# Second biases through TensorE into the attention's output bank, and a new order of the routing

## The chip, the cores and the metric

One core of a Trainium2 chip. The metric is the device time of one execution in microseconds (us); lower is better. Engines: TensorE (PE) multiplies matrices and writes PSUM, which has eight banks; VectorE (DVE) and ScalarE (ACT) do elementwise work and read PSUM; GpSimd (POOL) does elementwise work and issues the transfers with computed rows; SyncE (SP) issues most other transfers. Each engine works through its own list in order, and they wait for each other by semaphores.

## The reference

For 2048 tokens of 128 features (8 sequences of 256), with one layer norm shared by both branches:

```
xn  = layernorm(x)
out = x + linear_attention(xn) + moe(xn)

linear_attention: 16 heads of 8; phi(z) = elu(z) + 1
  Q, K, V = xn@Wq, xn@Wk, xn@Wv; Kv = phi(K)^T V; K1 = sum phi(K)
  (phi(Q) Kv) / (phi(Q) K1 + 1e-6), then @ Wo

moe: probs = softmax(xn @ gate_w^T + gate_b), top 2 of 8 experts
  h_e = relu(xn @ w1[e] + b1[e]); y_e = h_e @ w2[e] + b2[e]
  sum over the two chosen experts of prob_e * y_e
```

Everything is fp32; w1 is 128x256 and w2 256x128 for each expert.

## The kernel before

The tokens make 16 tiles of 128. The execution has these stages, which overlap.

**Routing.** x comes in five loads on SP's queue (parts of 2, 2, 4, 4, 4 tiles), followed there by constants, Wo and w2; identity, Wk|Wv|gate, Wq and the gate bias come on ScalarE's queue. VectorE takes the statistics, ScalarE the square roots, and three engines share the normalising (`xrow`). TensorE transposes, ScalarE copies back (`xT`), and `project_vg` (L923) makes V and the gate's logits for two tiles at a time. VectorE adds the gate bias, finds the top two (`top_two`, L642 and L645), and names the pair of experts (`find_pair`, L653 to L658, four tiles at a time). `rank_rows` (L948 to L955) counts on TensorE, in bf16, how many tokens of each pair stand ahead; `pair_starts` (L674) and `places` (L681 to L690) make of it each token's row in an order sorted by pair. `late_gates` (L731 to L744) makes the shares of tiles 8 to 15 on VectorE; GpSimd makes those of the first eight.

**Dispatch.** GpSimd scatters the 16 tiles of normalised rows to DRAM by these rows (L444), each row with its token number and its eight gate shares; SP then loads them back sorted (`xs`).

**Attention.** Per block of four tiles: `project_k`, `project_q`, ScalarE's exponential, VectorE's `finish_k` (L751) and `finish_q` (L756), `keys_values` (L992), VectorE's `mask_kv` (L761), `numerator` (L1007), VectorE's `divide` (L770 to L777), `transpose_att` (L1018), and `project_out`: an identity matmul puts x into the output's bank (L1031), four products with Wo add to it (L1036). ScalarE copies the sum out (`copy_sum`, L540) and SP stores it to `out`. phi of a key or query is max(min(exp(z), 1), z + 1); the 1 in z + 1 is put into the bank by an opener of one row of ones in bf16 (L935 for keys, L969 for queries), and the exponential takes it out again with a bias of -1.

**Visits.** In the sorted order each tile meets few experts; 59 visits (tile, expert) bound all cases. `visits` (L695 to L704) finds on VectorE which visits there are, `order_visits` (L976 on TensorE, L708 and L710 on VectorE) and `make_table` (L980) order them, `keep_table` (L715) keeps a table of offsets that the engines load into registers eight at a time. A visit is `first_product` (L1067), ScalarE's ReLU with b1 (L552), `second_product` (L1080), and on VectorE `take_y` (L793), which adds b2 from SBUF, and `accumulate` (L801), which adds the gate share times y to `acc`. The visits go through three banks each. Weights w1 are loaded anew for each visit, six buffers deep; w2 with b2 beside it is held whole.

**End.** When a tile's visits are done, GpSimd adds its rows to `out` by token number (`give_back`, L459). Tile s waits for the first `BOUND[s]` accumulations: 8, 16, 23, 28, 33, 37, 40, 43, and then two more for each tile up to 59.

The lists are written out by hand. TensorE's around the change: all value projections with `rank_rows(0)` and `rank_rows(1)` among them, key 1, rank 2, query 0, rank 3, key 2, query 1, kv 0, key 3, query 2, two warm-up matmuls, kv 1, kv 2, numerator 0, query 3, kv 3, warm-ups, numerator 1, warm-ups, and so on. Warm-ups are matmuls whose result nobody reads.

Of the kernel before, what the change touches and what calls it, by code (L numbers as in the profile page):

```python
# [11 lines left out]
ALU = mybir.AluOpType  # L12
# [3 lines left out]
P = 128  # L16
# [61 lines left out]
def linear_attention_with_pair_sorted_experts(nc, x, ident_in_dram, wkvg, wq, wo, gate_b, w1b, w2, consts,  # L78
# [13 lines left out]
    W1ROW = H + KC  # L92
    WROW = KC * D + D
# [12 lines left out]
    LATE = slice(8, T)  # L106
# [8 lines left out]
    with ExitStack() as ctx:  # L115
# [13 lines left out]
        wo_f = sb("wo_f", [P, D])  # L129
        gate_bias = sb("gate_bias", [P, E])  # L130
        w2_all = sb("w2_all", [P, E * WROW])
        w1_now = sb("w1_now", [P, NW, W1ROW])
# [13 lines left out]
        qf = sb("qf", [P, T * P])  # L146
        kf = sb("kf", [P, T, D])
# [21 lines left out]
        y = sb("y", [P, 2, D])  # L169
# [35 lines left out]
        vg_ps = [banks[:, (2, 3, 4, 6)[b % 4], 0:R * (D + E)].rearrange("p (r n) -> p r n", r=R) for b in range(B)]  # L205
        k_ps = [banks[:, i, :].rearrange("p (t d) -> p t d", t=4) for i in (7, 1, 0, 7)]
        rank_ps = banks[:, 5, 0:(T + 1) * NP].rearrange("p (t c) -> p t c", c=NP)
        order_ps = banks[:, 6, 0:1]
        table_ps = banks[0:3, 6, P:P + NI]
        kv_ps = [banks[:, i, :] for i in (6, 1, 6, 7)]  # L210
        num_ps = [banks[:, 2:4, :] if k % 2 == 0 else banks[:, 0:2, :] for k in range(NBLK)]
        attT_ps = banks[:, 4, :]
        wo_ps = [banks[:, 5 if k % 2 == 0 else 7, :] for k in range(NBLK)]
        warm_ps = banks[:, 5, 0:P]
        xsT_ps = [banks[:, n % 2, :] for n in range(len(XGROUPS))]
# [6 lines left out]
        gate_b_in = sem("gate_b_in")  # L222
        wkvg_in = sem("wkvg_in")
# [48 lines left out]
        y_done = sem("y_done")  # L272
# [52 lines left out]

        def group_of_visit(i):

            return sum(min(i // 2, T - 1) >= a for a, _ in XGROUPS) - 1
# [10 lines left out]
        def _(sp):  # L339
# [22 lines left out]
            def load_w1(i, woff):  # L362

                if i >= NW:
                    sp.wait_ge(h_done, KC * (i - NW + 1))
                sp.dma_start(w1_now[:, i % NW, :], w1b[:, bass.ds(woff, W1ROW)]).then_inc(w1_in[i % NW], 16)

# [16 lines left out]
        def _(pool):  # L384
# [17 lines left out]
            def shift(g):  # L402
                ts = blk_tiles(g)
                pool.wait_ge(top_done, 4 * g + 4)
                nc.gpsimd.tensor_tensor(shifted[:, ts, :], top8[:, ts, :], top8[:, ts, 0:1].to_broadcast([P, 4, 8]),
                                        ALU.subtract).then_inc(shift_done, 1)

            def gate_values(g):
                ts = blk_tiles(g)
                pool.wait_ge(rexpsum_done, g + 1)  # L410
                nc.gpsimd.tensor_tensor(gate2[:, ts, :], expd[:, ts, 0:TOP],
                                        rexpsum[:, ts].unsqueeze(2).to_broadcast([P, 4, TOP]), ALU.mult
                                        ).then_inc(gate2_done, 1)
                pool.wait_ge(gate2_done, g + 1)
                pool.wait_ge(chosen_done, g + 1)
                nc.gpsimd.tensor_tensor(gated[:, ts], chosen[:, ts],
                                        gate2[:, ts, :].unsqueeze(3).to_broadcast([P, 4, TOP, E]), ALU.mult
                                        ).then_inc(gated_done, 1)
                pool.wait_ge(gated_done, g + 1)
                nc.gpsimd.tensor_tensor(xrow[:, ts, D + 1:D + 1 + E], gated[:, ts, 0, :], gated[:, ts, 1, :], ALU.add  # L420
                                        ).then_inc(row_done, 1)
# [9 lines left out]
            def dispatch(t):  # L431
# [4 lines left out]
                if g < 2:  # L436
                    pool.wait_ge(row_done, g + 1)
# [30 lines left out]
            shift(0)  # L468
            shift(1)
            gate_values(0)  # L470
            gate_values(1)
# [9 lines left out]
        def _(act):  # L481
            nc.scalar.dma_start(ident_t[:], ident_in_dram).then_inc(ident_in, 16)
            nc.scalar.dma_start(wkvg_f[:], wkvg).then_inc(wkvg_in, 16)
            nc.scalar.dma_start(wq_f[:], wq).then_inc(wq_in, 16)
            nc.scalar.dma_start(gate_bias[:], gate_b.partition_broadcast(P)).then_inc(gate_b_in, 16)
# [23 lines left out]
            def exp_gates(g):  # L509
                if g < 2:  # L510
                    ts = blk_tiles(g)
                    act.wait_ge(shift_done, g + 1)
                    nc.scalar.activation(expd[:, ts, :], shifted[:, ts, :], ACT.Exp).then_inc(exp_done, 1)
# [4 lines left out]
            def copy_v(b):  # L518
                act.wait_ge(logits_done, b + 1)
                nc.scalar.copy(vext[:, R * b:R * b + R, 0:D], vg_ps[b][:, :, 0:D]).then_inc(v_done, 1)  # L520
# [54 lines left out]
            exp_gates(1)  # L575
            exp_k(0)
            for b in range(4, 7):
                copy_v(b)
            exp_k(1)
            copy_v(7)  # L580
            exp_q(0)
            exp_k(2)
            exp_gates(2)
# [3 lines left out]
            exp_q(3)  # L587
# [607 lines left out]
```

## Time and profile before

| | |
|---|---|
| median of 3 runs | 120.92 us (119.16 to 121.91) |
| the profiled execution's own time | 118.78 us |
| its span, first to last instruction | 117.0 us |
| busy in it: TensorE | 101.4 us (87%) |
| VectorE, ScalarE, GpSimd | 68.6, 60.5, 51.0 us |
| granted TensorE clock, mean | 0.973 |

The durations below come from the one profiled execution, whose own time is below the median. A busy TensorE is not TensorE at its peak: matmuls are pipelined and their ends are modelled, so the distance between starts says what one costs in a row. Rows of a timeline merge neighbours of one kind: the start, the time they cover, and their number. In brackets stands the idle time of the engine before it and what ended it.

### The profile page before, as it was taken

The page shows a single profiled execution, that of the slowest core. Times are in us where ns is not written, and L with a number is a line of the kernel's source. Part 1 is how long each engine was busy: PE and PEld are TensorE (multiplying, and loading weights), DVE is VectorE, ACT ScalarE, POOL GpSimd, SP SyncE. Part 2 cuts the span into 40 slices and gives each one's busy share as a digit, 9 for nine tenths or more (in the row PEclk, how much of TensorE's full clock was granted, in tenths as well). Part 3 has the DMA queues.
Part 4 walks back from the last instruction along what each step waited for, and adds up shares of the span by engine and source line. Part 5 has one row for each costly group of instructions (what it writes and reads, how often), then busy time and mean ns, then how long its engine had stood idle before and what let it go on. Part 6 is the DMA issues. An engine that isn't in the chain of part 4 may idle for free.

```text
span 117.0 us, 3091 instructions
## 1 busy us (share of the span) xinstructions
PE 101.4 (87%) x771; PEld 90.5 (77%) x771; DVE 68.6 (59%) x287; ACT 60.5 (52%) x171; POOL 51.0 (44%) x66
## 2 busy tenths in 40 slices
PE   6947989999797899989899999999999999999100
PEld 6946867667676777679899999999999999989000
DVE  0858988997719945011565556647567566574600
ACT  0657996444020221549466677776677667755000
POOL 5005800467777778011000403114505557887870
PEclk9999999999999999999999999999999999999955
DMA  3998000001111114999944665757577768962522
GB/s 93 279 339 365 11 0 6 0 24 48 54 63 57 48 55 128 250 252 346 311 110 127 131 165 145 174 136 171 162 162 161 185 154 165 198 112 23 45 22 25
DMA packets 16656, 15.52 MB, mean 133 GB/s; under 512 B 1920, under 2 KB 16256, under 8 KB 16512
## 3 DMA queue, kind: packets, MB, share of 16 engines
q1 hardware_dynamic: 13248, 12.88, 37.8%
q0 software_dynamic: 2816, 2.18, 12.9%
q10 hardware_dynamic: 576, 0.27, 0.8%
q8 instruction: 7, 0.11, 0.4%
q14 instruction: 9, 0.07, 0.2%
HBM read 12.09 MB, written 3.23 MB: 131 GB/s over the span
## 4 chain that ended last, share of the span: by engine, by line
issue 28%; PE 24%; POOL 19%; DVE 11%; DMA 10%; ACT 2%; POOLq 2%; SPq 1%; DVEq 0%
POOL out L459 19%; DMA x_tok<-in_x 5%; DMA out<-res 4%; PE banks L970 4%; PE banks L1031 3%; PE banks L1036 3%; PE banks L939 3%; PE banks L992 3%; PE banks L1007 2%; POOLq L115 2%; DVE att L777 1%; PE banks L923 1%; DVE idx L645 1%; PE banks L1018 1%; PE banks L969 1%
## 5 line engine op out<-in xcount | busy, mean ns | idle before, releaser
L552 ACT ACTIVATE h<-banks,w_now 128x128 f32<-128x128 f32 x118 | 36.9, 365 | 17.7 <-PE banks L1067 17.7
L459 POOL DMA_INDIRECT out<-acc,token x16 | 25.1, 1570 | 33.7 <-DVE acc L801 32.4
L1067 PE MATMUL banks<-xsT,w_now 128*128 x236 | 36.5, 278 | 0.7 <-DMA w_now<-in_w1b 0.4
L1080 PE MATMUL banks<-w_all,h 128*128 x236 | 36.1, 277 | 0.0
L1067 PEld LDWEIGHTS banks<-xsT,w_now 128*128 128x128 f32 x236 | 30.9, 192 | 1.4 <-issue 1.2
L1080 PEld LDWEIGHTS banks<-w_all,h 128*128 128x128 f32 x236 | 31.0, 192 | 0.3 <-issue 0.2
L793 DVE TENSOR_TENSOR y<-banks,w_all 128x128 f32<-128x128 f32 x59 | 17.2, 292 | 22.4 <-PE banks L1080 13.5
L801 DVE SCALAR_TENSOR_TENSOR acc<-y,xs,acc 128x128 f32 x59 | 20.7, 352 | 1.1 <-DVE y L793 0.9
L444 POOL DMA_INDIRECT sorted_dram<-xrow,slot x16 | 15.9, 991 | 5.3 <-issue 4.6
L895 PE MATMUL banks<-ones 128*128 128x128 f32 x42 | 7.4, 337 | 1.1 <-POOL ones L387 1.1
L895 PEld LDWEIGHTS banks<-ones 128*128 128x128 f32 x42 | 7.0, 250 | 1.5 <-POOL ones L387 1.1
L535 ACT COPY attT<-banks 128x512 f32<-128x512 f32 x4 | 2.3, 586 | 11.1 <-PE banks L1018 11.1
L530 ACT ACTIVATE qf<-banks,minus_one 128x512 f32<-128x512 f32 x4 | 2.8, 688 | 7.2 <-PE banks L970 7.2
L923 PE MATMUL banks<-wkvg_f,xT 128*128 128x136 f32 x32 | 5.0, 288 | 1.6 <-ACT xT L507 1.5
L609 DVE BATCH_NORM_STATS2 stats<-x_tok 128x6 f32<-128x128 f32 x16 | 3.6, 281 | 4.7 <-DMA x_tok<-in_x 4.5
L1007 PE MATMUL banks<-kv,qf 128*128 128x144 f32 x32 | 4.8, 294 | 1.6 <-DVE qf L756 1.6
L923 PEld LDWEIGHTS banks<-wkvg_f,xT 128*128 128x128 f32 x32 | 4.2, 190 | 2.3 <-issue 1.2
L1007 PEld LDWEIGHTS banks<-kv,qf 128*128 128x128 f32 x32 | 4.1, 190 | 2.1 <-issue 1.0
L1036 PEld LDWEIGHTS banks<-wo_f,attT 128*128 128x128 f32 x32 | 4.1, 191 | 2.1 <-issue 1.2
L396 POOL TENSOR_TENSOR xrow<-x_tok,mean_var 128x256 f32<-128x256 f32 (+1 forms) x3 | 1.6, 541 | 7.8 <-DVE rstd L617 7.8
L992 PEld LDWEIGHTS banks<-vext,kf 128*128 128x128 f32 x32 | 4.2, 190 | 1.0 <-issue 1.0
L786 DVE COPY xsT<-banks 128x256 f32<-128x256 f32 (+1 forms) x2 | 1.1, 554 | 6.1 <-PE banks L1050 6.1
(99 smaller groups left out, 115.4 us busy)
## 6 DMA issues: line engine op xcount, KB each, us to landing
w_now<-in_w1b SPq DMA_DIRECT2D x59, 129.0 KB, 2.7
w_all<-in_w SPq DMA_DIRECT2D x1, 1536.0 KB, 9.2
out<-res SPq DMA_DIRECT2D x4, 256.0 KB, 5.0
xs<-sorted_dram SPq DMA_DIRECT2D x3, 276.0 KB, 4.7
x_tok<-in_x SPq DMA_DIRECT2D x3, 256.0 KB, 6.1
xs<-sorted_dram SPq DMA_DIRECT2D x2, 138.0 KB, 3.3
x_tok<-in_x SPq DMA_DIRECT2D x2, 128.0 KB, 2.5
sorted_dram<-xrow,slot POOLq DMA_INDIRECT x16, 2.3
```

The lines of the kernel that those rows point to most:

```text
L444: nc.gpsimd.indirect_dma_start(out=sorted_dram, out_offset=bass.IndirectOffsetOnAxis(ap=slot[:, t:t + 1], axis=0), in_=xrow[:, t, :], in_o ...
L459: nc.gpsimd.indirect_dma_start(out=out_rows, out_offset=bass.IndirectOffsetOnAxis(ap=token[:, s:s + 1], axis=0), in_=acc[:, s * D:(s + 1) ...
L552: nc.scalar.activation(h[:, i % NH, c, :], h_ps[i % NHP][:, c * P:(c + 1) * P], ACT.Relu, bias=w1_now[:, i % NW, H + c:H + c + 1]).then_in ...
L793: nc.vector.tensor_tensor(y[:, i % 2, :], y_ps[i % NYP], w2_all[:, bass.ds(woff + KC * D, D)], ALU.add).then_inc(y_done, 1)
L801: nc.vector.scalar_tensor_tensor(out=mine, in0=y[:, i % 2, :], scalar=xs[:, bass.ds(goff, 1)], in1=mine, op0=ALU.mult, op1=ALU.add).then_i ...
L895: last = nc.tensor.matmul(warm_ps, ones[:], ones[:], start=True, stop=True)
L923: last = nc.tensor.matmul(vg_ps[b][:, r, :], xT[:, (R * b + r) * P:(R * b + r + 1) * P], wkvg_f[:, D:KVG], start=True, stop=True)
L992: last = nc.tensor.matmul(kv_ps[k][:, 256 * b:256 * b + NV], kf[:, t, :], vext[:, t, :], start=(r == 0), stop=(r == 1))
L1007: last = nc.tensor.matmul(num_ps[k][:, j // 2, (j % 2) * NV:(j % 2 + 1) * NV], qf[:, t * P:(t + 1) * P], kv[:, t // 2, :], start=True, sto ...
L1036: last = nc.tensor.matmul(wo_ps[k][:, j * P:(j + 1) * P], attT[:, t * P:(t + 1) * P], wo_f[:], start=False, stop=(j == 3))
L1067: last = nc.tensor.matmul(h_ps[i % NHP][:, c * P:(c + 1) * P], w1_now[:, i % NW, c * P:(c + 1) * P], xsT[:, bass.ds(toff, P)], start=True, ...
L1080: last = nc.tensor.matmul(y_ps[i % NYP], h[:, i % NH, c, :], w2_all[:, bass.ds(woff + c * D, D)], start=(c == 0), stop=(c == KC - 1))
```

## The change

- b2 leaves the visits: `take_y` is gone, and `accumulate` reads the product in PSUM. In its place the gate shares (tokens x experts) are written a second time (`gates`), transposed on TensorE four tiles at a time (`transpose_gates`), copied out by ScalarE (`copy_gatesT`), and multiplied in `project_out` with a block-diagonal b2 of 32 rows x 512 columns: one more fp32 product for each block, into the bank that already holds x.
- Queries have no opener: phi is min(exp(z), 1) + relu(z), with the ReLU as a second ScalarE operation for each block.
- Logits are taken for four tiles at a time, pairs named in groups of 8, 4 and 4 tiles, and the gate values of the first eight tiles in one step. The statistics of x's last two parts are taken in halves.
- Orders: see the lists in the diff. All `rank_rows` come after the value projections. The table of visits is made among the keys and queries, no longer between the divisions. ScalarE copies the last sum before the first sorted rows.
- Wq and the gate bias move from ScalarE's queue to SP's, behind the constants. Five of 21 warm-ups go.

```diff
@@ SP
             sp.dma_start(cst[:], consts).then_inc(consts_in, 16)
+            sp.dma_start(gate_bias[:], gate_b.partition_broadcast(P)).then_inc(gate_b_in, 16)
+            sp.dma_start(wq_f[:], wq).then_inc(wq_in, 16)
             sp.dma_start(wo_f[:], wo).then_inc(wo_in, 16)
+            sp.dma_start(b2_f[:], b2_blocks).then_inc(b2_in, 16)
             sp.dma_start(w2_all[:], w2).then_inc(w2_in, 16)
@@ ScalarE
-                nc.scalar.activation(qf[:, blk_cols(k)], q_ps[k], ACT.Exp, bias=minus_one[:, 0:1]
-                                     ).then_inc(qexp_done, 1)
+                nc.scalar.activation(qf[:, blk_cols(k)], q_ps[k], ACT.Exp).then_inc(qexp_done, 1)
+                nc.scalar.activation(q_relu[:, blk_cols(k)], q_ps[k], ACT.Relu).then_inc(qexp_done, 1)
...
+            def copy_gatesT():
+                act.wait_ge(gatesT_done, 1)
+                nc.scalar.copy(gatesT[:], gatesT_ps).then_inc(gatesT_copied, 1)
@@ VectorE: the visits
-            def take_y(i, woff):
...
-                nc.vector.tensor_tensor(y[:, i % 2, :], y_ps[i % NYP], w2_all[:, bass.ds(woff + KC * D, D)], ALU.add
-                                        ).then_inc(y_done, 1)
...
-                nc.vector.scalar_tensor_tensor(out=mine, in0=y[:, i % 2, :], scalar=xs[:, bass.ds(goff, 1)], in1=mine,
+                nc.vector.scalar_tensor_tensor(out=mine, in0=y_ps[i % NYP], scalar=xs[:, bass.ds(goff, 1)], in1=mine,
                                                op0=ALU.mult, op1=ALU.add).then_inc(acc_done, 1)
@@ VectorE: its list from the naming of the last pairs
             find_pair(2)
+            shares()
+            choose(0)
             late_shift()
-            finish_k(0)
             pair_starts()
             places(1, slice(0, 4))
+            finish_k(0)
+            finish_k(1)
             places(2, slice(4, T))
-            finish_k(1)
             mask_kv(0)
             finish_q(0)
-            choose(2)
-            choose(3)
+            choose(1)
             late_gates()
             finish_k(2)
+            visits()
             mask_kv(1)
             finish_k(3)
+            order_visits()
             finish_q(1)
             mask_kv(2)
+            keep_table()
+            divide(0)
             finish_q(2)
             mask_kv(3)
             finish_q(3)
-            divide(0)
             divide(1)
-            visits()
             divide(2)
-            order_visits()
-            keep_table()
             divide(3)
@@ TensorE
             def order_visits():
                 pe.wait_ge(table_step, 4)
-                pe.wait_ge(kvmask_done, 3)
+                pe.wait_ge(slot_done, 2)
...
             def project_out(k):
...
                 nc.tensor.matmul(wo_ps[k].rearrange("p (t d) -> p t d", t=4), ident_t[:], x_tok[:, blk_tiles(k), :],
                                  start=True, stop=False)
+                nc.tensor.matmul(wo_ps[k], gatesT[:, k * P:(k + 1) * P], b2_f[:], start=False, stop=False)
                 pe.wait_ge(attT_copied, k + 1)
@@ TensorE: its list from the last value projection
             project_vg(7)
+            rank_rows(0)
             project_k(1)
+            rank_rows(1)
+            project_q(0)
             rank_rows(2)
-            project_q(0)
-            rank_rows(3)
             project_k(2)
             project_q(1)
             keys_values(0)
             project_k(3)
             project_q(2)
-            warm_up(2, after=2)
+            order_visits()
             keys_values(1)
+            project_q(3)
+            make_table()
             keys_values(2)
             numerator(0)
-            project_q(3)
             keys_values(3)
-            warm_up(2)
+            transpose_gates()
             numerator(1)
-            warm_up(3)
+            warm_up(3, where=late_warm_ps)
             transpose_att(0)
             numerator(2)
-            order_visits()
             project_out(0)
             transpose_att(1)
-            make_table()
             numerator(3)
             project_out(1)
```

## Rows read from the trace of the kernel before

**Rows 1.** Busy time by stretch of the visits: engines, clock, DMA share, GB/s

```profile
60.00:80.00 20.00, 20.00 (x178) 19.98 (x179) 12.24 (x43) 13.56 (x44) 4.59 (x3) 1.00 0.60 147
```

**Rows 2.** VectorE's timeline: start, us, engine line op; accumulations of visits 42 and 58

```profile
96.22 0.35 DVE L801 SCALAR_TENSOR_TENSOR acc<-y,xs,acc 128x128 f32 x1
...
110.92 0.35 DVE L801 SCALAR_TENSOR_TENSOR acc<-y,xs,acc 128x128 f32 x1 [0.23 <-DVE acc L801]
```

**Rows 3.** TensorE's timeline: first visits, the seventh's first product, visit 42's second

```profile
51.79 1.12 PE L1067 MATMUL banks<-xsT,w_now 128*128 x8
...
57.76 0.71 PE L1067 MATMUL banks<-xsT,w_now 128*128 x4 [0.39 <-DMA w_now<-in_w1b]
...
93.55 0.61 PE L1080 MATMUL banks<-w_all,h 128*128 x4
```

**Rows 4.** GpSimd's timeline: scatters of tiles 7, 14 and 15

```profile
96.85 1.55 POOL L459 DMA_INDIRECT out<-acc,token  x1 [1.18 <-DVE acc L801]
...
110.17 1.56 POOL L459 DMA_INDIRECT out<-acc,token  x1 [0.41 <-DVE acc L801]
112.03 1.55 POOL L459 DMA_INDIRECT out<-acc,token  x1 [0.30 <-issue]
```

**Rows 5.** TensorE's timeline from the first ranking to the sorted rows

```profile
14.34 0.36 PE L948 MATMUL banks<-zero_bf,ones_bf 128*128 128x476 bf16 x1
...
15.29 0.62 PE L923 MATMUL banks<-wkvg_f,xT 128*128 128x136 f32 x4
...
18.46 0.38 PE L935 MATMUL banks<-ones_bf 1*128 1x512 bf16 x1
...
21.79 0.39 PE L935 MATMUL banks<-ones_bf 1*128 1x512 bf16 x1
...
28.67 2.13 PE L992 MATMUL banks<-vext,kf 128*128 128x144 f32 x16
31.65 1.22 PE L1007 MATMUL banks<-kv,qf 128*128 128x144 f32 x8 [0.85 <-DVE qf L756]
...
36.46 1.22 PE L1007 MATMUL banks<-kv,qf 128*128 128x144 f32 x8 [0.79 <-DVE qf L756]
...
40.29 0.38 PE L976 MATMUL banks<-visited,cst 128*128 128x1 f32 x2 [0.52 <-DVE visited L704]
...
44.17 1.02 PE L1031 MATMUL banks<-x_tok,ident 128*128 128x512 f32 x2
45.03 1.05 PE L1036 MATMUL banks<-wo_f,attT 128*128 128x128 f32 x8
...
50.78 0.38 PE L1050 MATMUL banks<-ident,xs 128*128 128x128 f32 x2
```

**Rows 6.** All engines' timeline: GpSimd takes the first sorted rows

```profile
50.63 0.19 POOL L451 CAST token<-xs 128x2 uint32<-128x2 f32 x1 [4.26 <-DMA xs<-sorted_dram]
```

**Rows 7.** VectorE's timeline: end of the third part's statistics, start of the fourth's

```profile
6.45 0.36 DVE L612 BATCH_NORM_AGGREGATE mean_var<-stats 128x2 f32<-128x6 f32 x4
8.26 0.87 DVE L609 BATCH_NORM_STATS2 stats<-x_tok 128x6 f32<-128x128 f32 x4 [1.44 <-DMA x_tok<-in_x]
```

**Rows 8.** VectorE's timeline: scan of pairs, third key finish, second mask, table of visits

```profile
22.45 0.21 DVE L674 TENSOR_TENSOR_SCAN start_of<-ones,banks 128x28 f32<-128x28 f32 x1
...
28.05 0.68 DVE L751 SCALAR_TENSOR_TENSOR kf<-kf,banks 128x512 f32<-128x512 f32 x1
29.86 0.46 DVE L761 TENSOR_TENSOR kv<-banks,cst 128x288 f32<-128x288 f32 x1 [1.13 <-PE banks L992]
...
39.25 0.23 DVE L695 TENSOR_SCALAR ends_in<-start_of,cst 128x28 f32<-128x28 f32 x1
```

**Rows 9.** Busy time by stretch after the last matmul; TensorE's granted clock after POOL's column

```profile
108.50:109.00 0.50, 0.02 (x1) 0.00 (x0) 0.49 (x2) 0.00 (x0) 0.50 (x1) 1.00 1.09 100
...
110.00:110.50 0.50, 0.00 (x0) 0.00 (x0) 0.40 (x2) 0.00 (x0) 0.33 (x1) 1.00 0.46 17
110.50:111.00 0.50, 0.00 (x0) 0.00 (x0) 0.27 (x2) 0.00 (x0) 0.50 (x1) 0.66 0.99 111
```

More of the change, by code:

```diff
@@ L324, in normalised, with pairs_known @@
             return [sum(len(n) for n in norm[:i + 1]) for norm in (NORM_DVE, NORM_ACT, NORM_POOL)]
+        def pairs_known(t):
+            return sum(t >= a for a, _ in PAIR_GROUPS)
         def group_of_visit(i):
@@ L423, in fill_rows @@
+                nc.gpsimd.tensor_tensor(gates[:, EARLY, :], gated[:, EARLY, 0, :], gated[:, EARLY, 1, :],
+                                        ALU.add).then_inc(gates_done, 1)
             def fill_rows():
@@ L587, in _ @@
             exp_q(3)
+            copy_gatesT()
             copy_attT(0)
@@ L605, in _, with statistics @@
         def _(dve):
-            def statistics(i):
+            def statistics(i, half=None):
+                a, b = PARTS[i]
+                if half is not None:
+                    a, b = a + 2 * half, a + 2 * half + 2
                 dve.wait_ge(x_in[i], 16)
-                for t in range(*PARTS[i]):
+                for t in range(a, b):
                     nc.vector.bn_stats(stats[:, t, :], x_tok[:, t, :]).then_inc(stats_done, 1)
-                for t in range(*PARTS[i]):
+                for t in range(a, b):
                     dve.wait_ge(stats_done, t + 1)
@@ L745, in late_gates @@
                                         ).then_inc(row_dve_done, 1)
+                nc.vector.tensor_tensor(gates[:, LATE, :], gated[:, LATE, 0, :], gated[:, LATE, 1, :], ALU.add
+                                        ).then_inc(gates_dve_done, 1)
             def finish_k(k):
@@ L889, in _, with warm_up @@
         def _(pe):
-            def warm_up(times, after=0):
+            def warm_up(times, where=warm_ps):
                 pe.wait_ge(ones_set, 1)
-                if after:
-                    pe.wait_ge(slot_done, after)
                 for _ in range(times):
-                    last = nc.tensor.matmul(warm_ps, ones[:], ones[:], start=True, stop=True)
+                    last = nc.tensor.matmul(where, ones[:], ones[:], start=True, stop=True)
                 last.then_inc(pe_warm, 1)
@@ L951, in rank_rows @@
                 pe.wait_ge(pair_done, g + 1)
[L952 to L954 removed]
+                a, b = PAIR_GROUPS[g]
+                nc.tensor.matmul(rank_ps[:, a:b, :], before_bf[:], of_pair[:, a:b, :], start=False, stop=False)
+                for t in range(a, b):
                     last = nc.tensor.matmul(rank_ps[:, t + 1:T + 1, :], ones_bf[:, 0:P],
@@ L994, in keys_values, with transpose_gates @@
                 last.then_inc(kv_done, 1)
+            def transpose_gates():
+                pe.wait_ge(table_done, 1)
+                pe.wait_ge(gates_done, 1)
+                pe.wait_ge(gates_dve_done, 1)
+                for k in range(NBLK):
+                    last = nc.tensor.transpose(gatesT_ps[:, k * P:(k + 1) * P],
+                                               gates[:, blk_tiles(k), :].rearrange("p t e -> p (t e)"), ident_t[:])
+                last.then_inc(gatesT_done, 1)
             def numerator(k):
```

244 lines of the change are left out of this document (114 added, 130 removed).

## The prediction

> **What bounds the kernel now.** I read the table by stretches first, then the engines' timelines. The execution has two halves, and each has its own bound.
>
> The visits, from 51.8 us on: TensorE is busy for 20.00 of 20.00 us, with 178 instructions [rows 1]. A visit is eight of them, so it takes 20.00 / 22.25 = 0.90 us. VectorE, with a bias add and an accumulation for each visit, must be read against that. Counted back from the last, the accumulation of visit 42 (of 0 to 58) starts at 96.22 [rows 2], its second product on TensorE already at 93.55 [rows 3]. With 0.61 us for the product and 0.35 for the accumulation, VectorE's result comes 96.57 - 94.16 = 2.4 us after TensorE's. TensorE's pace is not slowed by it, but GpSimd's is: the scatter of tile 7 needs visits 0 to 42 and starts 0.28 after that accumulation, at 96.85; the last one starts at 112.03 [rows 4]. Back to back one takes 1.86 us (110.17 to 112.03), eight make 14.9 of these 15.2 us. So the end is set by GpSimd's queue, and that by visit 42.
>
> The attention, up to 51.8: TensorE's last product ends at 50.78, where the transposes of the sorted rows start [rows 5]; the first sorted rows have landed at 50.63 [rows 6]. Two chains arrive together. Whatever lengthens TensorE's one moves the visits; shortening the dispatch alone gives nothing.
>
> **The change, part by part.** All times are on the profiled execution's own clock.
>
> *Visits and end.* The bias add goes, and one of VectorE's three register loads with it. VectorE then finishes an accumulation some 0.5 us after TensorE's product: 0.14 to start and 0.36 to run. The accumulation from PSUM is not in the trace; bounds are the 0.35 us from SBUF [rows 2] and that plus another half, which moves the result by 0.2. I take the near one. Tile 7's scatter starts 2.4 - 0.5 = 1.9 earlier, and eight scatters back to back lose the 0.25 of pauses between them: -2.15. Nothing at the end can take more, since GpSimd then waits for nothing but itself.
>
> *Front.* Two small loads move from ScalarE's queue to behind x on SP's, and the 1.5 MB of w2 starts three issues later. VectorE had finished the third part's statistics by 6.81 and waited for x's fourth load until 8.26, 1.44 us [rows 7]. With less beside it that load can land before 6.8; bounds are a gain of 1.4 and none, and I take the first. The Trainium skill (DMA: Bandwidth & Descriptors, Issuing engines are not separate DMA queues) says that transfers started by different engines run on the same DMA engines and interleave; by that rule the moved loads did hold x up, and the gain is 1.4, without it none. No run here shows it yet.
>
> The halved statistics give back some 0.1 of it, as ScalarE's next square root waits for both halves. More is lost on TensorE: ranking now stands behind all value projections. Before, these end at 18.46 and the last ranking at 21.79, 3.33 us with a key and a query projection between. Now the first half of the ranking, 0.95 us for its first group (14.34 to 15.29) and about 0.6 for its second, comes in there too, and one query opener goes, 0.39 as the key's at 21.79 has the same shape [rows 5]: 3.33 + 1.55 - 0.4 = 4.5. So ranking ends at 18.46 - 1.4 + 0.1 + 4.5 = 21.65, and VectorE's scan, at 22.45 before [rows 8], starts at 21.85: 0.6 earlier. Dispatch gains this 0.6 and no more.
>
> *The wait that the new order brings.* Instruction order on TensorE is now: second query projection, kv(0), third key and query projections, ordering of visits, kv(1). The ordering matmul waits for VectorE's visit table, and behind it in TensorE's queue stand kv(1), the fourth query, kv(2) and all numerators. VectorE's list up to there: from the scan to the end of the third key finish 6.2 us before (22.45 to 28.05, and 0.6) [rows 8], now with the first key finish inside it (0.6) and a second sum of the gates (0.2); then the table and its hand-over to TensorE, 1.04 (39.25 to 40.29) [rows 5, 8]. 21.85 + 6.2 + 0.8 + 1.0 = 29.85. TensorE is there at 21.65 + 1.4 + 0.95 + 1.0 + 1.35 + 0.95 = 27.3 (key, query, kv, key, query) and waits some 2.6 us.
>
> Then the two engines alternate. Ordering to 30.1; VectorE's mask 1.19 after kv(1)'s start (28.67 to 29.86) at 31.3; mask, key finish and order step 1.45, to 32.7; table matmul 0.2; kv(2) at 32.95, numerator(0) 1.0 later. The first division ends 2.8 after that numerator's start, 36.75, and two query finishes and a mask, 1.6, put the fourth query at 38.3. Numerator(1) waits for it: 38.45, against 36.46 [rows 5]. That is +2.0, although the front gave 0.6. The extra ReLU of the queries costs nothing while ScalarE idles there.
>
> *TensorE's own work after it.* From numerator(1) to the end, before: 50.78 - 36.46 = 14.3. Out of it go the wait of 0.52 for the table at 40.29, its two matmuls (0.45) and two short waits for copies (0.2), which the longer groups hide. In come four second-bias products. The trace has none: 32 rows, 512 columns, fp32. The nearest rows are x's product, 128 rows and the same columns and type, 0.86 us (44.17 to 45.03) [rows 5], and the bf16 opener of one row, 0.39. I take 0.86, since type and columns agree; so 4 x 0.86 = 3.45, at the least 1.6. The gates' four transposes fall into the wait before numerator(1). Sum: 14.3 - 1.15 + 3.45 = 16.6, and the end is at 38.45 + 16.6 = 55.05, 4.3 late. The last sum now leaves PSUM before the sorted rows' copy: +0.1.
>
> *Given back.* The seventh visit waited for its weights (57.76, 0.39 marked, about 0.6 of TensorE's pace) [rows 3]; base stores now stand apart from it: -0.6, or nothing.
>
> **Sum.** +4.3 + 0.1 - 0.6 - 2.15 = +1.65 us on a span of 117.0, so 118.65; the profiled run's own time of 118.78 becomes 120.4. That run was 2.1 below the median of 120.92; on the median the forecast is 122.6, or +1.4%. A measurement of this kernel tells about 2% from no change.
>
> **Rivals.**
> *TensorE's clock falls in the new wait.* After the last matmul, ending at 108.5, the clock stood at 1.00 until 110.5; in the next half us its mean is 0.66, so it fell to the lower level (1.2 GHz) early in it [rows 9], some 2.1 us on. The wait of 0.85 us before 31.65 [rows 5] left it at 2.4 GHz. A wait of 2.6 lies beyond both. The ordering and kv(1) at half rate add 1.25 on the chain: 123.9. Against it: VectorE a little quicker makes the wait shorter. It decides if the wait stays as long as walked. [...]
> *x lands no earlier.* The fourth load's lateness then has another cause than the moved loads, and everything up to the visits is 1.4 later: 124.0. For it: the load is itself behind three others of x. With the clock falling too: 125.3.
> *TensorE's stretch is not what sets the visits.* If the second-bias products and the waits fill time in which TensorE had nothing to do, the dispatch sets the start, 0.6 earlier: -0.6 + 0.1 - 0.6 - 2.15 = -3.25, or 117.7. For it: the two chains arrive within 0.2 us now. Against it: from 40.29 to 50.78 TensorE hardly waits. It needs an end at 50.1 or before.
>
> **How the numbers follow.** Forecast as summed 0.38; clock 0.25; x late 0.18; both 0.09; dispatch sets it 0.10. The two middle rivals lie at +2.5%, so with an error of a us either way about two thirds of their 0.43 are slower by over 2%, and so is a quarter of the forecast's share; with both together that makes 0.48. Faster by over 2%: 0.09. Within: 0.43. The low end lies where half of the last rival's gain comes, 119.5; the high end at both rivals, 125.4.
>
> **What would show it.** Right: VectorE's fourth statistics start by 7 us; TensorE idles before the ordering matmul for over 2 us; numerator(1) near 38.5; second-bias products 0.86 us apart; first product of the visits near 56.2; tile 7's scatter about 1 us after its product, and eight more without pauses. Wrong: a first product before 53, or an idle TensorE before the sorted rows' transposes; second-bias products well below 0.86; scatters that still wait for accumulations.

## The result, and the profile after

The changed kernel is slower: 124.15 us median (122.60 to 125.44, four runs) against 120.81, a ratio of 1.045, 95% interval 1.037 to 1.054. On another chip, with more runs, it was 1.036 (1.029 to 1.044). Ratios leave disturbed executions out; medians don't.

| | before | after |
|---|---|---|
| profiled execution's own time | 118.78 us | 124.28 us |
| its span | 117.0 us | 122.5 us |
| granted TensorE clock, mean | 0.973 | 0.955 |
| TensorE busy | 101.4 us | 106.5 us |
| VectorE busy | 68.6 us | 53.3 us |
| ScalarE, GpSimd busy | 60.5, 51.0 us | 62.6, 51.2 us |

The two profiled spans are 5.5 us apart, the medians 3.3: the profiled execution of before was 2.0 below its median, that of after stands at its own. What a typical execution of before loses against the profiled one, no trace here shows.

VectorE lost 15.3 us of work, as meant, and TensorE took on 5.1. What that did to the end is read from TensorE's timeline, from the ordering of the visits to their first product (start, us, engine line op, out<-in, count, idle before and what ended it); lines of after are the changed kernel's own:

```profile
26.45 1.02 PE L970 MATMUL banks<-xT,wq_f 128*128 128x512 f32 x2
29.89 0.59 PE L976 MATMUL banks<-visited,cst 128*128 128x1 f32 x2 [2.42 <-DVE visited L725]
30.34 2.27 PE L992 MATMUL banks<-vext,kf 128*128 128x144 f32 x8
32.40 1.92 PE L970 MATMUL banks<-xT,wq_f 128*128 128x512 f32 x2
...
34.53 2.17 PE L992 MATMUL banks<-vext,kf 128*128 128x144 f32 x8
36.54 1.14 PE L1016 MATMUL banks<-kv,qf 128*128 128x144 f32 x8
...
41.03 1.22 PE L1016 MATMUL banks<-kv,qf 128*128 128x144 f32 x8 [1.93 <-DVE qf L779]
...
52.02 1.02 PE L1042 MATMUL banks<-x_tok,ident 128*128 128x512 f32 x2
52.98 1.12 PE L1044 MATMUL banks<-b_f,gatesT 32*128 32x512 f32 x2
54.03 1.16 PE L1048 MATMUL banks<-wo_f,attT 128*128 128x128 f32 x8
55.02 0.60 PE L1027 MATMUL banks<-ident,att 128*128 128x128 f32 x4
...
58.46 0.60 PE L1062 MATMUL banks<-ident,xs 128*128 128x128 f32 x4
59.72 1.15 PE L1079 MATMUL banks<-xsT,w_now 128*128 x8 [0.66 <-issue]
```

The ordering matmul (L976) waits 2.42 us for VectorE's table. Behind it kv(1), at 30.34, takes 2.06 us to the next start, and kv(2), at 34.53, takes 2.01; such a product of eight matmuls had taken 1.0 before. Numerator(1) starts at 41.03, against 36.46 before [rows 5], and the first product of the visits at 59.72, against 51.79 [rows 3].

Busy time by stretch says why the two are twice as long. The columns are the stretch and its length, then PE, PEld, DVE, ACT and POOL busy with their counts, then TensorE's granted clock, DMA share and GB/s:

```profile
28.00:29.00 1.00, 0.00 (x0) 0.00 (x0) 1.00 (x4) 0.60 (x2) 0.88 (x1) 1.00 0.25 79
29.00:30.00 1.00, 0.11 (x1) 0.11 (x1) 0.73 (x4) 0.00 (x0) 0.81 (x1) 0.81 0.27 79
30.00:31.00 1.00, 1.00 (x5) 1.00 (x6) 0.00 (x0) 0.00 (x0) 0.69 (x2) 0.50 0.20 71
...
35.00:36.00 1.00, 1.00 (x6) 1.00 (x6) 0.00 (x0) 0.44 (x1) 0.70 (x2) 0.50 0.00 0
36.00:37.00 1.00, 1.00 (x8) 1.00 (x7) 0.26 (x1) 0.00 (x0) 0.80 (x1) 0.78 0.21 71
```

TensorE is idle from 27.47 on (26.45 + 1.02). A mean of 0.81 over 29 to 30 says that the clock went to its lower level, 1.2 GHz, at 29.6: 2.15 us after the last matmul, and 0.3 before the wait was over. It stayed there until about 36.4, well into steady work.

The weight loads of the same stretch (PEld, TensorE's second record) tell of the products at the output bank:

```profile
52.98 0.29 PEld L1044 LDWEIGHTS banks<-b_f,gatesT 32*128 32x128 f32 x2 [0.76 <-issue]
54.03 0.97 PEld L1048 LDWEIGHTS banks<-wo_f,attT 128*128 128x128 f32 x8 [0.76 <-issue]
```

A load of the second bias's 32 rows, and then the first of Wo's 128, each start only with their product; nothing is loaded while the product ahead runs. In the kernel before, Wo's first weights were loaded at 44.60, while x's product ran from 44.17 to 45.03:

```profile
44.60 0.19 PEld L1036 LDWEIGHTS banks<-wo_f,attT 128*128 128x128 f32 x1 [0.24 <-issue]
```

Start to start, in the changed kernel, x's product takes 0.96 us (52.02 to 52.98), the second bias's 1.05, Wo's four 0.99. Before, x's took 0.86 [rows 5].

GpSimd's timeline: the first sorted rows, the scatter of tile 7 and the last one.

```profile
48.64 0.19 POOL L467 CAST token<-xs 128x2 uint32<-128x2 f32 x1 [2.28 <-DMA xs<-sorted_dram]
...
102.04 1.55 POOL L475 DMA_INDIRECT out<-acc,token  x1 [1.17 <-DVE acc L816]
...
117.66 1.56 POOL L475 DMA_INDIRECT out<-acc,token  x1 [0.31 <-issue]
```

The sorted rows are there at 48.64, 2.0 earlier than before [rows 6] and ten before TensorE gets to them. From the first product to tile 7's scatter it takes 42.32 us, against 45.06 before (51.79 to 96.85) [rows 3, 4]: the visits did get 2.74 quicker. So the whole loss lies ahead of 59.72: +7.93 there, -2.74 in the visits, +0.44 among the last scatters (15.62 against 15.18), -0.1 after them, +5.5 in all.

### The profile page after: what moved, and what is told of

Read it like the earlier page. It is cut to its first block, busy times and chain, and to the rows that moved or that the text cites. A ratio compares the mean times of both kernels' runs of the same rounds, so it can differ in the third digit from the quotient of the medians.

```text
span 122.5 us, 2893 instructions
## 1 busy us (share of the span) xinstructions
PE 106.5 (87%) x768; PEld 92.2 (75%) x768; DVE 53.3 (44%) x218; ACT 62.6 (51%) x175; POOL 51.2 (42%) x63
## 4 chain that ended last, share of the span: by engine, by line
issue 28%; PE 28%; POOL 18%; DVE 11%; DMA 5%; ACT 4%; POOLq 2%; SPq 1%
POOL out L475 18%; DMA x_tok<-in_x 4%; PE banks L1048 4%; PE banks L992 3%; PE banks L1044 3%; PE banks L1016 3%; PE banks L1042 3%; PE banks L922 3%; PE banks L970 2%; DMA out<-res 2%; ACT xrow L513 2%; DVE kf L773 2%; POOLq L115 2%; DVE qf L779 1%; PE banks L1027 1%
## 5 line engine op out<-in xcount | busy, mean ns | idle before, releaser
L1079 PE MATMUL banks<-xsT,w_now 128*128 x236 | 36.4, 277 | 1.1 <-issue 0.7
L816 DVE SCALAR_TENSOR_TENSOR acc<-banks,xs,acc 128x128 f32 x59 | 20.7, 350 | 35.9 <-PE banks L1092 34.9
L460 POOL DMA_INDIRECT sorted_dram<-xrow,slot x16 | 16.5, 1034 | 6.3 <-issue 4.6
L894 PE MATMUL banks<-ones 128*128 128x128 f32 x32 | 6.4, 375 | 1.1 <-POOL ones L403 1.1
L894 PEld LDWEIGHTS banks<-ones 128*128 128x128 f32 x32 | 6.0, 286 | 1.1 <-POOL ones L403 1.1
L992 PE MATMUL banks<-vext,kf 128*128 128x144 f32 x32 | 6.7, 372 | 0.0
L992 PEld LDWEIGHTS banks<-vext,kf 128*128 128x128 f32 x32 | 6.1, 262 | 0.7 <-DVE kf L773 0.4
L541 ACT ACTIVATE qf<-banks 128x512 f32<-128x512 f32 x4 | 2.4, 597 | 6.2 <-PE banks L970 6.1
L970 PE MATMUL banks<-xT,wq_f 128*128 128x512 f32 x8 | 5.0, 716 | 0.0
```

The lines of the kernel that those rows point to most:

```text
L460: nc.gpsimd.indirect_dma_start(out=sorted_dram, out_offset=bass.IndirectOffsetOnAxis(ap=slot[:, t:t + 1], axis=0), in_=xrow[:, t, :], in_o ...
L816: nc.vector.scalar_tensor_tensor(out=mine, in0=y_ps[i % NYP], scalar=xs[:, bass.ds(goff, 1)], in1=mine, op0=ALU.mult, op1=ALU.add).then_in ...
L894: last = nc.tensor.matmul(where, ones[:], ones[:], start=True, stop=True)
L970: nc.tensor.matmul(q_ps[k], wq_f[:], xT[:, blk_cols(k)], start=True, stop=True).then_inc(q_done, 1)
L992: last = nc.tensor.matmul(kv_ps[k][:, 256 * b:256 * b + NV], kf[:, t, :], vext[:, t, :], start=(r == 0), stop=(r == 1))
L1079: last = nc.tensor.matmul(h_ps[i % NHP][:, c * P:(c + 1) * P], w1_now[:, i % NW, c * P:(c + 1) * P], xsT[:, bass.ds(toff, P)], start=True, ...
```

## The experiments

Two causes were in question: the clock that fell in the new wait, and the second-bias product, dearer than the 0.86 that the forecast took. The rival to the first was that the new order costs this much at any clock; to the second, that one such product more costs about what x's does.

**Fill the wait.** The changed kernel with ten warm-up products that start when VectorE has done the places, so that TensorE works through the wait. The cut shows the call; `after=2` makes the first of them wait for the places.

```diff
             project_q(2)
+            warm_up(10, after=2)
             order_visits()
             keys_values(1)
```

> The changed kernel with ten warm-up matmuls (2.2 us) put ahead of the ordering matmul, after slot_done 2, so that TensorE works through most of its wait; the wait itself stays. Theory (the clock): in the changed kernel the clock fell at the end of the 2.42 us wait, and kv(1), the fourth query and kv(2) then ran at half rate. Filled, kv(1) takes 1.0 us again instead of 2.06, numerator(1) starts near 38.5 instead of 41.03, the first product of the visits near 57.1 instead of 59.72, ratio to before about 1.024. Rival (the half clock is hidden under VectorE's work, the stretch is long because of its order alone): numerator(1) stays near 41, ratio 1.045.

Measured: 121.59 us, ratio 1.013 (1.005 to 1.022). TensorE's timeline, and the clock of the stretches that were at half rate:

```profile
27.16 2.39 PE L896 MATMUL banks<-ones 128*128 128x128 f32 x20
29.75 0.38 PE L978 MATMUL banks<-visited,cst 128*128 128x1 f32 x2 [0.19 <-DVE visited L725]
29.99 1.23 PE L994 MATMUL banks<-vext,kf 128*128 128x144 f32 x8
...
38.55 1.22 PE L1018 MATMUL banks<-kv,qf 128*128 128x144 f32 x8 [1.93 <-DVE qf L779]
...
57.24 1.15 PE L1081 MATMUL banks<-xsT,w_now 128*128 x8 [0.66 <-issue]
```

```profile
29.00:30.00 1.00, 0.81 (x8) 0.62 (x7) 0.62 (x3) 0.00 (x0) 0.95 (x1) 1.00 0.28 79
30.00:31.00 1.00, 1.00 (x10) 1.00 (x10) 0.00 (x0) 0.00 (x0) 0.70 (x1) 1.00 0.20 71
```

The ordering matmul comes as late as ever, at 29.75, but the clock holds, kv(1) takes 1.07 and numerator(1) starts at 38.55: 2.48 us earlier, and so is the first product. The fallen clock cost 2.5 us of this execution; the lateness of the table alone cost what the forecast had walked.

**Both once more on one chip.** The ratios above are from two chips, so the unaltered kernel and the filled one were run side by side.

> The changed kernel unaltered, beside the one with ten warm-ups in the wait, so that both are measured on one chip against the same runs of the kernel before. If the fallen clock is a cost of this kernel and not of the chip it was first timed on, its ratio is again 1.03 to 1.045, its runs lie at a granted clock of 0.955 to 0.985, those with the lower clock being the longer ones, and numerator(1) starts near 41.0 in a profile whose clock fell. If the first chip made the difference, the ratio is 1.013, that of the kernel with warm-ups.

> The changed kernel with ten warm-up products in the wait, on the chip of the unaltered one: ratio to the kernel before 1.013, granted clock 0.98 to 0.99 in every run, numerator(1) at 38.5, and by the clock theory 2 to 3 us below the unaltered kernel; by the rival, that the first chip made the difference, level with it.

Measured: 1.036 (1.029 to 1.044) for the unaltered kernel, 1.020 (1.014 to 1.026) for the filled one. The difference is 1.7%, or 2.0 us, a little under the 2.5 of the traces. It is the kernel and not the chip. But several expectations fell. The filled kernel's ratio is above 1.013, and its clock wasn't held in every run: one at 0.968 had it whole through kv(1) and kv(2), and lost it at 38.6 us, behind the next wait, of 1.93. The unaltered kernel's runs don't get longer as their mean clock gets lower (122.72 us at 0.967, 124.0 at 0.975, 123.91 at 0.958), and its numerator(1) did not start near 41.0. TensorE's timeline, four rows of the unaltered kernel and then one of the filled:

```profile
29.67 0.38 PE L976 MATMUL banks<-visited,cst 128*128 128x1 f32 x2 [2.42 <-DVE visited L725]
...
39.33 1.22 PE L1016 MATMUL banks<-kv,qf 128*128 128x144 f32 x8 [1.93 <-DVE qf L779]
40.39 1.39 PE L894 MATMUL banks<-ones 128*128 128x128 f32 x6
...
59.68 1.15 PE L1079 MATMUL banks<-xsT,w_now 128*128 x8 [0.66 <-issue]
...
38.57 2.18 PE L1018 MATMUL banks<-kv,qf 128*128 128x144 f32 x8 [1.93 <-DVE qf L779]
```

The unaltered kernel's clock fell twice: at 30.2, 0.6 us after work had resumed, until about 33.7 (the mean over 30 to 31 is 0.62), and again at 40.5, behind the wait of 1.93, until about 43.9. The first fall cost 0.78 to numerator(1) (39.33 for 38.55), the second 1.66 from there to the first product (20.35 for 18.69): 2.44 together, again. The filled kernel's late fall cost it the same 1.66, its first product starting at 58.92. So the fill takes away the first fall, and not a fall behind the next wait.

**Put kv(1) into the wait.** Real work in place of warm-ups.

```diff
             project_q(2)
-            order_visits()
             keys_values(1)
+            order_visits()
             project_q(3)
```

> The changed kernel with kv(1) ahead of the ordering matmul on TensorE, nothing else. Theory (the wait blocks kv(1), and VectorE then waits for kv(1)): both are gone, the clock holds because TensorE idles for only about 1.4 us, VectorE's second mask starts right behind its table near 29.9 instead of 32.65, numerator(1) near 37.0, first product near 55.6, ratio to before about 1.012. Rival (the wait costs only through the clock): as with the filled wait, numerator(1) near 38.5, ratio 1.024. Second rival (neither matters): 41.0 and 1.045.

Measured: 121.54 us, ratio 1.011 (1.000 to 1.022). The wait shrank to 1.45 and the clock held in this profile; numerator(1) came at 36.85 and the first product at 55.54, both as expected. Yet the span equals that of the filled kernel, 119.3, although its visits began 1.7 us earlier. The table of waits of TensorE over the visits (us in total, times, longest) has what took it:

```profile
PE banks L1079 <- DMA w_now<-in_w1b: 1.0, 2, 0.6
PE banks L1079 <- issue: 0.7, 1, 0.7
PE banks L1079 <- ACT h L567: 0.4, 1, 0.4
```

The filled kernel had only the middle one. Two visits waited for their weights and one for ScalarE's ReLU, 1.4 us together. The earlier front was given back in this execution, most of it to waits for w1. That does not follow from an early front: with both repairs, and in the better version and its second form (all below), the visits begin at 55.66, 53.17 and 50.00, and there TensorE waits for no weights. Why they come late in one execution and not in another is not settled.

**Second bias padded to 128 rows.** Gate shares and b2 blocks get zeros up to 128 rows; the result is the same, and all products into the bank then have 128 rows.

```diff
-        b2_f = sb("b2_f", list(b2_blocks.shape))
+        b2_f = sb("b2_f", [P, b2_blocks.shape[1]])
...
-        gatesT = sb("gatesT", [4 * E, NBLK * P])
+        gatesT = sb("gatesT", [P, NBLK * P])
```

> The changed kernel with the second-bias product padded by zeros from 32 to 128 rows (gates in 128 columns per block, 128 rows of b2 blocks): the same columns, more rows. Theory (the change from 128 rows to 32 and back exposes the weight loads): x, second bias and Wo follow each other every 0.86 to 0.89 us, an output group with its transpose takes 2.65 instead of 3.00, the first product of the visits is 1.4 us earlier, ratio to before about 1.034. Rival (a third weight change in the bank costs this whatever its rows): groups stay at 3.00, ratio 1.045.

Measured: 121.66 us, ratio 1.012 (1.003 to 1.020). In its profile x, second bias and Wo of a block take 2.61 together, where it was 3.00 (52.02 to 55.02); the rows are shown below, from the kernel with both repairs, which has the same 2.61. A fourfold larger product is the cheaper one. By luck the clock did not fall here after the same wait, of 2.43, and numerator(1) started at 38.42; this profile alone would have credited the padding with that too, and so may the time, which is below the 1.034 expected.

**Without the second-bias products.** b2 is left out of the output; all else as in the changed kernel.

```diff
-                nc.tensor.matmul(wo_ps[k], gatesT[:, k * P:(k + 1) * P], b2_f[:], start=False, stop=False)
```

> The changed kernel without the four second-bias products: b2 is left out of the output, gates and their transposes stay. Theory (a product costs more than its columns, 1.19 us with what its neighbours lose, by the distance of the output groups of 3.00 against 1.81): the first product of the visits comes 4.7 us earlier, near 55.0, and the ratio to before is about 1.006. Rival (it costs its 512 columns, 0.86 us): 3.45 earlier, 56.3, ratio 1.017. The clock still falls in both.

Measured: 118.90 us, ratio 0.986 (0.975 to 0.996). TensorE's timeline, numerator(1), one group and the end:

```profile
40.84 1.22 PE L1016 MATMUL banks<-kv,qf 128*128 128x144 f32 x8 [1.94 <-DVE qf L779]
...
49.33 1.02 PE L1042 MATMUL banks<-x_tok,ident 128*128 128x512 f32 x2
50.19 1.14 PE L1047 MATMUL banks<-wo_f,attT 128*128 128x128 f32 x8
...
53.44 0.60 PE L1061 MATMUL banks<-ident,xs 128*128 128x128 f32 x4
```

The clock fell here too (numerator(1) at 40.84), but from there to the end it takes 12.60 us, where the changed kernel took 17.43 (41.03 to 58.46). Four products cost 4.83, or 1.21 each: 0.35 more than x's product, of the same type and columns, takes in this trace (49.33 to 50.19). The first product came at 54.70, as expected; the ratio is below the 1.006 expected, and what gave the rest is not known, as the unaltered kernel was not timed on that chip.

**Both repairs.** Ten warm-ups in the wait and the padded product.

> The changed kernel with both repairs at once: ten warm-up products in the wait ahead of the ordering matmul, and the second-bias product padded to 128 rows. If the fallen clock and the change of row counts are the two whole causes of what the forecast missed, numerator(1) starts at 38.4 to 38.6, the four groups of the output projection are 2.6 each with a transpose, the first product of the visits is at 55.4 to 55.8 (the forecast said 56.2, the changed kernel showed 59.72), and the time is 1.5 to 2 below that of the warm-ups alone (121.6 there): 119.6 to 120.1, level with the kernel before. The rival, that from here on the weights' arrival or the scatters set the rest of the visits: first product as early, but the time stays at 120.6 to 121.6.

Measured: 120.88 us, ratio 1.009 (1.005 to 1.014), span 118.0. TensorE's timeline:

```profile
29.73 0.38 PE L983 MATMUL banks<-visited,cst 128*128 128x1 f32 x2 [0.20 <-DVE visited L729]
...
38.53 1.22 PE L1023 MATMUL banks<-kv,qf 128*128 128x144 f32 x8 [1.93 <-DVE qf L784]
...
48.75 1.02 PE L1049 MATMUL banks<-x_tok,ident 128*128 128x512 f32 x2
49.61 1.02 PE L1051 MATMUL banks<-b_f,gatesT 128*128 128x512 f32 x2
50.47 1.05 PE L1055 MATMUL banks<-wo_f,attT 128*128 128x128 f32 x8
...
54.40 0.60 PE L1069 MATMUL banks<-ident,xs 128*128 128x128 f32 x4
55.66 1.15 PE L1086 MATMUL banks<-xsT,w_now 128*128 x8 [0.66 <-issue]
```

x, second bias and Wo now follow each other after 0.86, 0.86 and 0.89, and the first product is at 55.66, 4.1 before that of the changed kernel. The two causes, 2.5 by the clock and 1.6 by the rows (57.24 to 55.66), are the whole miss of the front, which was 3.5, and half a us more. The time is another matter: 120.88 lies in the rival's range, not in 119.6 to 120.1. The rival's cause isn't seen in the profile, which took 120.15 us and in whose visits TensorE waits for no weights. The ten runs part by their granted clock: five at 0.989 or more took 119.6 to 120.8, five at 0.977 or less 121.0 to 122.3. So a clock that falls elsewhere is the likelier reason; no trace of those runs shows it. The intervals overlap, and timing alone doesn't part 1.009 from the filled kernel's 1.013 on its chip.

**The two gains alone, on the kernel before.** First the visits without a bias add (b2 is left out of the output), then Wq and the gate bias behind the constants on SP's queue.

```diff
-                dve.wait_ge(y_done, i + 1)
+                dve.wait_ge(l2_done, i + 1)
...
-                nc.vector.scalar_tensor_tensor(out=mine, in0=y[:, i % 2, :], scalar=xs[:, bass.ds(goff, 1)], in1=mine,
+                nc.vector.scalar_tensor_tensor(out=mine, in0=y_ps[i % NYP], scalar=xs[:, bass.ds(goff, 1)], in1=mine,
```

> The kernel before with the bias add left out of the visits: VectorE accumulates straight from PSUM, b2 is left out of the output, everything ahead of the visits is as before. Theory (GpSimd's scatters at the end wait for VectorE, which is 2.4 us behind TensorE at visit 42): tile 7's scatter comes about 43.1 us after the visits' first product instead of 45.06, the last scatter about 14.9 us after it; the span is 2.1 shorter, ratio about 0.982. Rival (the scatters' own time or the landing of the last one sets the end): ratio 0.995 to 1.00.

```diff
@@ SP
             sp.dma_start(cst[:], consts).then_inc(consts_in, 16)
+            sp.dma_start(gate_bias[:], gate_b.partition_broadcast(P)).then_inc(gate_b_in, 16)
+            sp.dma_start(wq_f[:], wq).then_inc(wq_in, 16)
@@ ScalarE
-            nc.scalar.dma_start(wq_f[:], wq).then_inc(wq_in, 16)
-            nc.scalar.dma_start(gate_bias[:], gate_b.partition_broadcast(P)).then_inc(gate_b_in, 16)
```

> The kernel before with the loads of Wq and the gate bias moved from ScalarE's queue to SP's, behind the constants, nothing else. Theory (they held x up): VectorE's statistics of x's fourth part start near 7.3 instead of 8.26, and all that follows, dispatch and attention, is 0.9 us earlier; ratio about 0.992. Rival (x's loads hold each other up): 8.2 as before, ratio 1.00.

Measured: 118.56 us, ratio 0.988 (0.983 to 0.993), and 117.84 us, ratio 0.988 (0.982 to 0.993). The first is worth 1.4 us rather than the 2.15 of the forecast. In its profile tile 7's scatter comes 44.77 after the first product (52.70 to 97.47), not the 43.1 expected; 1.2 of this are waits for loads of w1 in the visits, and the reason for the rest isn't settled. The last scatter follows after 14.89, as expected. The second gave somewhat more than expected, though its interval holds that too, and its VectorE timeline shows where it came from:

```profile
6.67 0.84 DVE L609 BATCH_NORM_STATS2 stats<-x_tok 128x6 f32<-128x128 f32 x4
...
7.96 0.86 DVE L609 BATCH_NORM_STATS2 stats<-x_tok 128x6 f32<-128x128 f32 x4
```

These are the statistics of the fourth and the fifth part. They don't wait for x any more, where the fourth load had been 1.44 late [rows 7]: the fourth start at 6.67 against 8.26, and the first product of the visits is at 50.79, 1.0 earlier than [rows 3].

**A better version.** Starting from the changed kernel: kv(1) stands ahead of the ordering; x doesn't go through TensorE at all, VectorE adds it where ScalarE copied the sum out; the three warm-ups behind numerator(1) go.

```diff
-                nc.tensor.matmul(wo_ps[k].rearrange("p (t d) -> p t d", t=4), ident_t[:], x_tok[:, blk_tiles(k), :],
-                                 start=True, stop=False)
-                nc.tensor.matmul(wo_ps[k], gatesT[:, k * P:(k + 1) * P], b2_f[:], start=False, stop=False)
+                nc.tensor.matmul(wo_ps[k], gatesT[:, k * P:(k + 1) * P], b2_f[:], start=True, stop=False)
@@ VectorE, in place of ScalarE's copy_sum
+                nc.vector.tensor_tensor(res[:, blk_tiles(k), :], wo_ps[k].rearrange("p (t d) -> p t d", t=4),
+                                        x_tok[:, blk_tiles(k), :], ALU.add).then_inc(res_done, 1)
```

Its first runs gave 116.41 us, ratio 0.974 (0.961 to 0.987), for some 0.975 expected. In their profile the first product came at 52.87 rather than near 51: the clock fell at 31.7, behind the ordering's wait of 1.44, and numerator(1) started at 38.55. It was run again beside a version that also has the padded product and seven warm-ups behind kv(1):

> The version with x added by VectorE once more, on the same chip as the one with padded product and held clock: 116.4 as before, ratio to the kernel before 0.974. In a profile whose clock doesn't fall after the ordering wait, numerator(1) would be at 36.5 to 37.0, in one where it falls at 38.5.

> The version with x added by VectorE, with the padded second-bias product and seven warm-up products between keys_values(1) and the ordering matmul. Clock and rows theory: the rate stays whole through keys_values(2), numerator(1) comes at 36.4 to 37.0 (38.55 in the profiled run of the version without these), a group with transpose takes about 1.75 to 2.2 instead of 2.58, end of the projection at 48.6 to 49.6, first product at 49.8 to 50.6 (52.87), and 113.5 to 114.5 in all (116.4). Rival, the rest of the visits is set by the weights' arrival and the queue of scatters: first product as early, but 115.5 to 116.5.

Measured: 116.28 us, ratio 0.972 (0.963 to 0.980), and 115.44 us, ratio 0.970 (0.961 to 0.979). TensorE's timeline of the second:

```profile
36.99 1.22 PE L1023 MATMUL banks<-kv,qf 128*128 128x144 f32 x8 [1.93 <-DVE qf L775]
...
48.92 0.73 PE L1065 MATMUL banks<-ident,xs 128*128 128x128 f32 x4
50.00 1.15 PE L1082 MATMUL banks<-xsT,w_now 128*128 x8 [0.35 <-issue]
```

Its first product is at 50.00, as expected, 3.17 before that of the version without padding and fill (53.17), and its span 112.9 against 115.3. The profile of the version without has numerator(1) at 37.19, and its clock falls behind that (last section). Timed, the two aren't told apart, and 115.44 lies above the 113.5 to 114.5 expected, next to the rival's 115.5. Both beat the kernel before by some 3%.

## Why the prediction was wrong in its verdict and right in its walk

The range held the time (124.15 in 119.5 to 125.4), but the forecast, 122.6 or +1.4%, lay within 2%, and the kernel is 4.5% slower. That the time fell into the range is in part luck: on the profiled executions' clock the forecast was 120.4 and the result 124.28, 3.9 off, and the medians hide 2.0 of it, since only that of before lay above its profile. (The low end, half of the last rival's gain, would be 119.3, not 119.5.) Two steps of the walk failed and made the miss. Step by step, on the profiled execution's clock; the last column is the kernel with both repairs:

| step | forecast | after | both repairs |
|---|---|---|---|
| VectorE's scan | 21.85 | 22.00 | |
| ordering matmul | 29.85 | 29.89 | 29.73 |
| from there to numerator(1) | 8.6 | 11.14 | 8.80 |
| numerator(1) to TensorE's end | 16.6 | 17.43 | 15.87 |
| end to first product | 1.15 | 1.26 | 1.26 |
| **first product of the visits** | **56.2** | **59.72** | **55.66** |
| first product to tile 7's scatter | 42.56 | 42.32 | 42.13 |
| tile 7's scatter to the last | 14.93 | 15.62 | 15.27 |

**The step that failed first: from the ordering matmul to numerator(1), walked at the full clock.** The forecast gave the fall a chance of 0.25, on the right rows: it had read 2.1 us from the last matmul to the fall [rows 9], and a wait of 2.6 to come. The fall came 2.15 after the last matmul. With these two numbers the fall was the likelier case, and the objection, that VectorE might be a little quicker, was worth 0.2 us and not enough; of four profiles with this wait, three show a fall in it or soon behind it. The rival's price was too small as well: 1.25, from the ordering and kv(1) alone. The lower level lasted from 29.6 to 36.4 and took in the fourth query and kv(2): 1.0 more for each kv, some on the query, 2.5 in all. The Trainium skill (TensorE: Matmul & The Clock Gate, Why this matters for your kernels) advises against idle gaps between bursts of matmuls, but names longer ones than this wait of 2.42 us; here the clock fell 2.15 us after the last matmul, at a price of 2.5 us, and the measurement decides.

**The second: "I take 0.86, since type and columns agree".** A product of 32 rows between products of 128 costs 1.21, as the run without them shows, because weights are no longer loaded ahead across the change of rows: 0.76 of idle weight loading stands ahead of each, and x's and Wo's products become 0.1 longer with it. Padded, it costs (15.87 - 12.60) / 4 = 0.82. The lower bound of the forecast's cost was a row with fewer rows and another type; the upper bound was missing. The same page says that one product with few rows takes as long as one with 128; beside neighbours with other rows, this trace shows 1.05 against 0.86 from start to start. The rest of this stretch was 0.55 shorter than walked, which hid part of the miss.

**What held.** The place and length of the new wait: the ordering matmul within 0.04, the wait 2.42 for "some 2.6". The tail: -2.74 + 0.44 = -2.3 in the visits and scatters, for -2.15 and -0.6. VectorE's accumulation from PSUM costs what it did from SBUF:

```profile
L816 DVE SCALAR_TENSOR_TENSOR acc<-banks,xs,acc 128x128 f32 x59 | 20.7, 350 | 35.9 <-PE banks L1092 34.9 <-DVE acc L816 1.0
```

Of its idle time 34.9 us were ended by TensorE: VectorE now follows TensorE directly. That the scatters would run without pauses was not quite so: three waited 0.47 to 0.64, two of them behind a stall of TensorE by a ReLU.

**x's load** came earlier: the fourth statistics start at 7.30 without a wait for it, against 8.26 [rows 7], 1.0 of the 1.4 forecast, as now the third part is 0.65 late instead. So "x lands no earlier" is out. The run with nothing but the two moved loads agrees with the rule of the Trainium skill (DMA: Bandwidth & Descriptors, Issuing engines are not separate DMA queues) that queues interleave: 1.2% of the time.

**"TensorE's stretch is not what sets the visits"** is out too: the sorted rows lie ready for ten us, and each us taken from TensorE's stretch brought the first product forward by as much.

With the wait filled, the change costs 1.3 to 2.0%, about the +1.4% of the forecast. That is partly luck: its products cost 1.4 more than taken, and other parts less. The change itself is a trade: 15 us of VectorE, of which the end saw 2.3, for 4.8 of TensorE, all on the path.

## What to carry to other kernels

Before work is moved to the engine that sets the pace, price it at that engine, with its neighbours: an fp32 product with other rows than those beside it cost 1.21 us, and 0.82 when padded to their 128. Where an order makes TensorE wait, compare the wait with the times after which traces show its clock falling (2.07 and 2.15 us after the last matmul here, and later behind waits of 1.44 and 1.93 in some executions), and count all that follows until the clock is seen back, not only the next product; work that is due anyway, or idle products, belong into such a wait, and the next wait has to be looked at too. And judge a front by the first product of the next stage as well as by the time, since the waits for weights in that stage differed from profile to profile (none to 1.9 us) and can hide what the front gained.

## What was not expected of the hardware

The same wait does not always bring the clock down. After 2.42 to 2.43 us it had fallen in the changed kernel and in the one without second-bias products; in the unaltered kernel on another chip it fell 0.6 us after work had resumed, and in the padded one not at all. Shorter waits could do it later: the first profile of the better version shows a fall 2.2 us after the ordering matmul, behind a wait of 1.44. In the second profile of the better version without fill it held through a wait of 1.45, and fell at about 37.8, 0.65 us after work had resumed behind the next wait, of 1.93. By stretch, columns as above:

```profile
36.00:37.00 1.00, 0.00 (x0) 0.00 (x0) 1.00 (x3) 0.00 (x0) 0.91 (x1) 1.00 0.84 262
37.00:38.00 1.00, 0.81 (x6) 0.84 (x7) 0.04 (x1) 0.00 (x0) 0.79 (x1) 0.92 0.77 160
38.00:39.00 1.00, 1.00 (x6) 0.99 (x5) 0.15 (x1) 0.00 (x0) 0.69 (x2) 0.50 1.00 339
```

In its second form, with fill, the same wait of 1.93 passed at 1.00. What decides between the two is not settled by these runs. So one profile is no proof that a clock holds; the times of four to ten runs were needed to see what a fill is worth.
